# Reordering the bank-sharing pieces in both cross attentions of a two-layer decoder

## What is computed

```python
# layer 0: 16 heads of 16
Q = (x @ Wq.T).reshape(B, xN, NUM_HEADS, HEAD_DIM)
KV = (z @ Wkv.T).reshape(B, zN, 2, NUM_HEADS, HEAD_DIM)
attn = softmax(einsum('bqhd,bkhd->bhqk', Q, K) * SCALE)
O = einsum('bhqk,bkhd->bqhd', attn, V).reshape(B, xN, DIM)
return O @ Wo.T
# layer 1: 16 heads of 64, the same form, with an output bias
```

## Time and profile before

| what | value |
|---|---|
| median of three runs | 3632.3 us |
| the profiled execution's own time | 3628.8 us |
| its span | 3627.0 us |
| mean granted TensorE clock | 0.967 |
| TensorE busy | 3279.1 us (90%) |
| weight loads busy | 2430.0 us (67%) |
| VectorE busy | 1890.2 us (52%) |
| ScalarE busy | 1664.0 us (46%) |
| GpSimd busy | 783.1 us (22%) |
| first cross attention, first and last maximum | 647.9 and 1275.6 us |
| second cross attention, first and last maximum | 2179.6 and 3219.4 us |
| second cross attention, 2204 to 3124 us | TensorE busy 889.08 of 920.00 us, granted clock 1.00 |

### The profile page before, as it was taken

One profiled execution on the slowest core, in us unless ns is written; L12 is line 12 of the kernel. 1 busy time (PEld: TensorE's weight loads), 2 busy tenths in 40 slices (PEclk: granted clock), 3 DMA queues, 4 the chain that ended last, 5 costly groups with the idle time before them and its releaser, 6 DMA issues. The chain is left out here.

```text
span 3627.0 us, 76508 instructions
## 1 busy us (share of the span) xinstructions
PE 3279.1 (90%) x24554; PEld 2430.0 (67%) x24555; DVE 1890.2 (52%) x5145; ACT 1664.0 (46%) x4616; POOL 783.1 (22%) x854
## 2 busy tenths in 40 slices
PE   5999998899999979899997979999999999979982
PEld 4777776566666656677775756767767777756761
DVE  3555555577777756222223644565655656653333
ACT  2555554566666621122221326666666666631220
POOL 0000000000000000333332110223323233234773
PEclk9999999899999989999998989999999999999996
DMA  8400000300000041211112010100000000114774
GB/s 271 133 0 0 0 0 13 136 8 10 10 8 10 6 140 50 65 31 30 29 25 54 0 50 7 30 28 20 18 9 15 13 11 13 43 48 113 219 203 126
DMA packets 141202, 181.21 MB, mean 50 GB/s; under 512 B 36156, under 2 KB 115001, under 8 KB 140108
## 3 DMA queue, kind: packets, MB, share of 16 engines
q1 hardware_dynamic: 89890, 134.89, 12.1%
q0 software_dynamic: 45760, 26.67, 4.6%
q10 hardware_dynamic: 5482, 18.73, 1.4%
HBM read 116.11 MB, written 103.61 MB: 61 GB/s over the span
## 5 line engine op out<-in xcount | busy, mean ns | idle before, releaser
L1247 DVE TENSOR_REDUCE e_nmx<-PS 128x1 f32<-128x361 f32 x416 | 221.3, 532 | 397.9 <-PE PS L1093 349.6
L1594 ACT ACTIVATE b_p<-PS,b_nmx 100x361 f32<-100x361 f32 x512 | 275.2, 568 | 163.4 <-DVE b_nmx L1681 163.4
L1093 PE MATMUL PS<-e_cT,e_qT 128*128 128x361 f32 x832 | 336.0, 486 | 0.0
L882 POOL DMA_INDIRECT slot_rows<-r_row,r_rows_now x256 | 256.3, 1001 | 360.4 <-DVE e_p L1254 306.0
L1198 ACT ACTIVATE e_pT<-PS 121x384 f32<-121x384 f32 (+1 forms) x416 | 198.6, 478 | 219.7 <-PE PS L1100 214.0
L1681 DVE TENSOR_REDUCE b_nmx<-PS 100x1 f32<-100x361 f32 x512 | 247.6, 526 | 90.7 <-PE PS L1442 88.8
L2587 PE MATMUL PS<-c_wgu,c_tile_xT 128*128 x912 | 290.2, 461 | 1.4 <-ACT c_tile_xT L2642 1.4
L1100 PEld LDWEIGHTS PS<-ident,e_p 128*121 128x121 f32 x1248 | 198.5, 185 | 102.2 <-ACT e_pT L1198 6.6
L1203 ACT ACTIVATE e_p<-PS,e_nmx 128x361 f32<-128x361 f32 x416 | 232.3, 559 | 36.3 <-DVE e_nmx L1247 36.2
L1449 PE MATMUL PS<-ident,b_p 100*121 100x100 f32 x1536 | 222.3, 281 | 6.6 <-PEq L191 4.2
L2587 PEld LDWEIGHTS PS<-c_wgu,c_tile_xT 128*128 128x128 f32 x912 | 169.6, 191 | 78.2 <-issue 3.3
(11 more groups left out here) (339 smaller groups left out, 6491.9 us busy)
## 6 DMA issues: line engine op xcount, KB each, us to landing
f_w<-in_f_W SPq DMA_DIRECT2D x64, 384.0 KB
slot_rows<-a_empty SPq DMA_DIRECT2D x1, 21504.0 KB, 64.9
f_xg<-slot_rows SPq DMA_DIRECT2D x64, 336.0 KB
c_wgu<-in_c_GU ACTq DMA_DIRECT2D x8, 1408.0 KB, 16.6
sum<-X SPq DMA_DIRECT2D x2, 3200.0 KB, 57.3
f_sums<-sum SPq DMA_DIRECT2D x16, 400.0 KB
b_cT<-in_ctx_T SPq DMA_DIRECT2D x32, 181.5 KB, 2.3
e_cT<-in_ctx_T SPq DMA_DIRECT2D x32, 181.5 KB, 2.4
```

The lines of the kernel that those rows point to most:

```text
L882: pool.indirect_dma_start(out=self.rows, in_=self.row[:, u, :], in_offset=None, out_offset=bass.IndirectOffsetOnAxis(ap=self.rows_now[:, u ...
L1093: sr.fill_done(pe.matmul(sr.at(f"s{m}", ROWS, CTX), qT[:, at:at + ROWS], cT[:, u, 0:CTX], start=True, stop=True), f"s{m}")
L1247: dve.tensor_reduce(nmx[:, m:m + 1], sr.at(f"s{m}", ROWS, CTX), AX.X, ALU.max, negate=True).then_inc(max_ready, 1)
L1594: sr.move_done(act.activation(p[:, g % 2, a, 0:CTX], sr.at(f"s{g}{a}", S, CTX), ACT.Exp, bias=nmx[:, g, a:a + 1]), f"s{g}{a}")
```

## The change

In both attentions no instruction is added or taken away; the order in which the engines issue them, and so the order in which pieces use the shared banks, is another.

First cross attention: the first piece of a slot now stands between the scores and `weigh`, the second between the two halves of `turn_probs`; the sixteen pieces are dealt anew to the slots. ScalarE's fourth exponential stands ahead of the copy of the second piece; the copies of the first piece stand behind the first exponential. The first probability copy stands behind the second exponential. On VectorE the copy of the first piece stands ahead of the fourth maximum, and the layer norm is split, statistics at slot 2 and the scaling at slot 3. A second, identical wait at the head of ScalarE's list is left out.

Second cross attention: tables `Q_AT` and `V0_AT`, and `add(0, i)` from slot 14 to slot 13.

```diff
-    Q_AT = {14: 0, 15: 1, 19: 2, 21: 3}
-    V0_AT = {17: (0,), 18: (1, 2), 20: (3,), 23: (4,), 25: (5,)}
+    Q_AT = {14: 0, 15: 1, 17: 2, 18: 3}
+    V0_AT = {10: 0, 19: 1, 20: 2, 21: 3, 23: 4, 25: 5}
...
-                        if this and n == 14:
+                        if this and n == 13:
                             dve.wait_ge(biased, i * 2 + 2)
                             add(0, i)
                         if prev and n in CHOOSE_AT:
...
-        mr = Ring(k, 7, 1).plan(["v10", "v12", "xT", "r0", "t0", "q", "k00", "y0", "v00", "k01", "v02", "r1",
-                                 "t1", "k10", "y1", "k11"])
+        mr = Ring(k, 7, 1).plan(["v10", "v12", "xT", "k00", "r0", "t0", "q", "k01", "y0", "v00", "v02", "k10",
+                                 "r1", "k11", "t1", "y1"])
...
                         if at:
                             scores(*at)
+
+                        if this and n == 0:
+                            values(1, 0, i)
+                        if nxt and n == 1:
+                            turn_x(i)
+                        if this and n == 2:
+                            turn_sums(0, i)
+                        if nxt and n == 3:
+                            queries(i)
+                        if this and n == 4:
+                            out(0, i)
+                        if nxt and n == 5:
+                            values(0, 2, i)
+                        if this and n == 6:
+                            turn_sums(1, i)
+                        if this and n == 7:
+                            turn_out(1, i)
+
                         at = ahead(n, WEIGHED, i, this, nxt)
                         if at:
                             weigh(*at)
...
                         if this and n == 0:
-                            values(1, 0, i)
+                            values(1, 2, i)
                         if nxt and n == 1:
-                            turn_x(i)
+                            keys(0, 0, i)
                         if this and n == 2:
                             turn_out(0, i)
                         if nxt and n == 3:
-                            keys(0, 0, i)
-                        if nxt and n in (4, 5):
-                            values(0, 2 * (n - 4), i)
-                        if this and n == 6:
-                            turn_out(1, i)
+                            keys(0, 1, i)
+                        if nxt and n == 4:
+                            values(0, 0, i)
+                        if nxt and n in (5, 6):
+                            keys(1, n - 5, i)
                         if this and n == 7:
                             out(1, i)
...
                         if at:
                             exponent(at[0], 0, at[1])
+                        if nxt and n == 1:
+                            move_x(i)
                         if nxt and n == 3:
-                            sr.wait_full(act, f"s{GROUPS - 1}{TILES_R - 1}", i)
+                            move_queries(0, i)
                             move_queries(1, i)
+                        if this and n == 7:
+                            move_out(1, i)
+                        if this and n in (1, 5):
+                            move_sums(n // 4, i)
+                        if at:
+                            exponent(at[0], 1, at[1])
                         if before:
                             move_probs(before[0], 0, before[1])
-                        if this and n == 1:
-                            move_sums(0, i)
-                        if this and n == 5:
-                            move_sums(1, i)
                         if at:
-                            exponent(at[0], 1, at[1])
                             exponent(at[0], 2, at[1])
+                            exponent(at[0], 3, at[1])
...
                         if before:
                             move_probs(before[0], 2, before[1])
-                        if at:
-                            exponent(at[0], 3, at[1])
...
+                        if this and n == 0:
+                            move_values(1, 0, i)
+                        if this and n in (2, 6):
+                            divide(n // 4, i)
+                        if this and n == 4:
+                            add(0, i)
+                        if nxt and n == 5:
+                            move_values(0, 2, i)
+                        if at:
+                            maximum(at[0], 3, at[1])
                         if before:
                             move_probs(before[0], 1, before[1])
-                        if at:
-                            maximum(at[0], 3, at[1])
...
                         if nxt and n == 2:
-                            norm(i + 2)
-                        if this and n == 3:
-                            add(0, i)
-                        if this and n == 5:
-                            divide(1, i)
+                            statistics(i + 2)
+                        if nxt and n == 3:
+                            apply(i + 2)
```

More of the change, by code:

```diff
@@ L950, in packed_cross_attention @@
         order += [(n, 2, f"q{r}.{j}") for n, j in Q_AT.items() for r in range(HT)]
-        order += [(n, 3, f"v0.{m}") for n, ms in V0_AT.items() for m in ms]
+        order += [(n, 3, f"v0.{m}") for n, m in V0_AT.items()]
         led = [name for _, _, name in order]
@@ L1143, in turn @@
                         if nxt and n in V0_AT:
-                            for m in V0_AT[n]:
-                                values(0, m, i + 1)
+                            values(0, V0_AT[n], i + 1)
                         if this and n in V1_AT:
@@ L1227, in turn @@
                         if nxt and n in V0_AT:
-                            for m in V0_AT[n]:
-                                move_values(0, m, i + 1)
+                            move_values(0, V0_AT[n], i + 1)
                         if this and n in V1_AT:
@@ L1541, in _ @@
                 turn_x(-1)
+                keys(0, 0, -1)
                 mr.pass_over(pe, "r0", "t0")
                 queries(-1)
-                keys(0, 0, -1)
+                keys(0, 1, -1)
+                scores(0, 0)
                 mr.pass_over(pe, "y0")
-                scores(0, 0)
                 values(0, 0, -1)
-                keys(0, 1, -1)
                 scores(1, 0)
@@ L1552, in _ @@
                     turn_probs(0, a, 0)
-                mr.pass_over(pe, "r1", "t1")
+                keys(1, 0, -1)
                 scores(2, 0)
                 weigh(0, 0)
-                keys(1, 0, -1)
-                mr.pass_over(pe, "y1")
+                mr.pass_over(pe, "r1")
                 for a in range(TILES_R):
                     turn_probs(1, a, 0)
+                keys(1, 1, -1)
                 scores(3, 0)
                 weigh(1, 0)
-                keys(1, 1, -1)
+                mr.pass_over(pe, "t1", "y1")
                 for a in range(TILES_R):
@@ L1699, in add, with statistics, apply @@
                                                    ALU.add), f"y{u}")
-                def norm(t):
-                    xs = [X[:, 2 * t + u, :] for u in range(2)]
-                    norm_statistics(dve, ln, Chain(norm_step, LN_STEPS), t, xs)
-                    norm_apply(dve, ln, t, xs)
+                def statistics(t):
+                    norm_statistics(dve, ln, Chain(norm_step, LN_STEPS), t, [X[:, 2 * t + u, :] for u in range(2)])
+                def apply(t):
+                    norm_apply(dve, ln, t, [X[:, 2 * t + u, :] for u in range(2)])
                 def turn(i, this, nxt):
@@ L1723, in turn @@
                             move_probs(before[0], 3, before[1])
-                        if this and n == 0:
-                            move_values(1, 2, i)
-                        if this and n == 1:
-                            divide(0, i)
                         if nxt and n == 2:
-                            norm(i + 2)
-                        if this and n == 3:
-                            add(0, i)
-                        if this and n == 5:
-                            divide(1, i)
+                            statistics(i + 2)
+                        if nxt and n == 3:
+                            apply(i + 2)
                 dve.tensor_reduce(parity[:], k.quarter_rows[:].rearrange("p (a r) -> p r a", r=PAR), AX.X, ALU.add)\
                    .then_inc(parity_made, 1)
-                norm(0)
+                statistics(0)
+                apply(0)
                 dve.wait_ge(prepared, PREPARED)
@@ L1746, in _ @@
                 move_probs(0, 3, 0)
-                norm(1)
+                statistics(1)
+                apply(1)
                 for a in range(TILES_R):
```

48 lines of the change are left out of this document (14 added, 34 removed).

## The result

The changed kernel takes 3657.62 us (median of 4 runs, 3653.89 to 3660.08), the kernel before 3628.47 (4 runs, 3623.47 to 3633.61). The ratio is 1.0079 with an interval of 1.0062 to 1.0095: slower, by 29 us. The prediction was 3626 with a range up to 3648; the result lies 10 us outside.

The account below looks back on a forecast made before the run. TensorE's order of work was taken to set the turn. First attention -30 us, second +25.5, sum -4.5 on 3628.8 = 3624.3; 3626 predicted for a median, own range 3612 to 3640, with rivals 3594 to 3648.

Parts of the forecast that it names:

- The list of places and sizes: First attention: waits left in the new order, slot by slot (slots 1, 2, 3 and 6), 1.33 us a turn together.
- I take 0.87: First attention: six transposes ahead of scores charged 0.87 us, bounds 0.78 and 0.97; eight slots give +0.86.
- +0.5 a turn: First attention: net charge in us for new neighbours on TensorE, transposes ahead of scores and pieces ahead of weighing; bounds 0 and 3.0.
- 3.83: First attention: us a turn that TensorE lost before the change, at ten places where bank 7's pieces came too close.
- the second rival: First attention: sixteen new borders a turn each show a 0.19 us load, total 3666, most likely near 3646; chance 0.18.
- The wait at queries 1: Second attention: TensorE waits 1.20 us because routing behind `add` delays slot 14's maximum and queries 1 need both banks.
- the one on r_key: Second attention, slot 18: queries 3 take rc's bank, which r_key frees, so they wait 1.74 us.
- the wait ahead of rc: Second attention, slot 17: rc needs bank 7 from query piece 2 at once, with VectorE 0.95 late; 1.76 us lost.
- the 4.7 us of waits: Second attention: new waits a turn, 1.20 + 1.76 + 1.74 = 4.70 in place of 2.79, so 1.91 us more.
- the upper bound of +35: Second attention: most the stage was to lose, in us, with every delay 0.3 us longer; forecast +25.5, lower bound 0.
- The first: Rival, second attention: VectorE not late at slot 17, or rc's bank free earlier; 3602 at its lower bound; chance 0.27.
- The third: Rival: first attention gains all 3.83 us a turn, second pays as worked out, -57 + 25.5 = 3601; chance 0.08.

## Why the prediction was wrong

- **First attention, the waits: right.** The list of places and sizes (0.24, 0.26, 0.19 and the small ones) came as laid out. Start to start, over the 0.71 us that is usual there, the places named lose 0.32 us in slot 1, 0.54 in slot 2, 0.35 in slot 3 and 0.17 in slot 6: 1.38 instead of 1.33.
- **First attention, the borders: over-charged.** The step "I take 0.87" for transposes ahead of scores measured 0.71 to 0.81, and its 0.71 is below the 0.78 that a slot's second six took in the order before. The +0.5 a turn was -0.3, as far as the turn shows: 39.07 - 36.28 = 2.79, against 3.83 - 1.38 = 2.45 by the waits alone. That makes the looped turns' gain 39 us; the other 5 of the 44 lie in the first stretch, which varies, and were not foreseen. The upper bound with a whole weight load at each border, and with it the rule of the Trainium skill that stands behind the second rival ("TensorE: Matmul & The Clock Gate", Part 3), is contradicted by these rows: a load for the 32-row scores, behind transposes of all rows, adds nothing like the 0.186 us of a load to the 0.71 that six transposes take anyway.
- **Second attention, the waits: right.** 67.6 us a turn were predicted. The kernel with its waits filled has 67.62, and so have the turns of the one with only rc's wait filled in which the clock held. The wait at queries 1 and the one on r_key have the causes that were named. Of the wait ahead of rc the cause was half named: putting routing ahead of `add` leaves 1.43 of it.
- **Second attention, what runs behind the waits: this step failed.** The sum gave every matmul its duration of before, at a granted clock of 1.00 ("The second cross attention is the same kind of stage", with "granted clock 1.00 on the page"), and took the 4.7 us of waits as plain time. They came as three within 13 us (2536.04 to 2549.29), and behind the second TensorE ran at 1.2 GHz for 6 to 7 us. That is 3.0 us a turn (70.6 against 67.6), 38 us in the stage, and it is more than the waits themselves added (1.9 a turn). Neither the upper bound of +35 nor a rival held it. With that term the sum is -30 + 26 + 38 = +34; the first attention's better 44 makes it +20, and the profiled spans differ by 25. So the first attention's error hid a part of this one. The first stretch of the second stage (3.8) is most of the remaining 5, and no run shows whether the change lengthened it.
- **The rivals.** The first (the second attention keeps its gain) failed as the text against it said, by bank parity. The second was on the right side for a reason that did not exist. The third had the first attention no nearer than the forecast (-44 lies midway between -30 and -57).
- **The sum.** -4.5 on the median of 3632.3 is 3627.8; the 3626 written is 1.8 below it, for no stated reason. Nothing hangs on it.

What is open: why the clock falls behind these waits and not behind the 1.22 and 0.80 of the kernel before, and why, with the same waits, it falls in some turns and not in others (five of thirteen with only rc filled, nine of thirteen with `add` back, none of the first three with the layer norm whole). No run separates the sum of the idle times from their spacing.

## What to carry to other kernels

Where a change adds waits on a TensorE that is otherwise busy, do not price them at their length: look whether they stand close together, and read the granted clock in windows of a few microseconds behind each; here that term was larger than the waits. To take a wait off one engine, look for the place in the serving engine's list that delays nothing else: the same `add` was worth 0.2 us a turn in slot 13 and 1.3 us at the head of slot 14. And to tell waiting from a lower clock, fill the idle time with matmuls that nobody reads: only the clock's share comes back.

## What the runs showed of the hardware

- The granted clock fell to 0.50 behind idle times of 1.05 and 1.59 us that ended 8 us apart, and was back at 1.00 some 7 us later, though a third of 1.35 us fell in between. One wait of 1.56 in each turn went with 0.92 to 0.96 in eleven looped turns of a stage (39 to 41 us each), and with 1.00 in the three ahead of them (38 us); 1.22 and 0.80 in a turn of 65.7 us left it at 1.00.
- Matmuls added in idle time made the kernel faster: 4.9 us of them in each turn, 38 us off the stage, at a granted clock of 1.00 where it had been 0.93 to 0.95 a turn.
- A weight load of 32 rows behind transposes of 100 rows cost nothing that can be read: 0.71 us at best for six transposes ahead of scores, the same as ahead of anything else.
